# Token mixer: four sequences' values in four quarters of TensorE's array, softmax denominators from halves that GpSimd adds

## What is computed

```python
q, k, v = jnp.split(qkv, 3, axis=1)              # each 128 x 32 x 512
scale = 1.0 / np.sqrt(np.sqrt(ch))
weight = jnp.einsum('bct,bcs->bts', q * scale, k * scale)
weight = jax.nn.softmax(weight.astype(jnp.float32), axis=-1)
h = jnp.einsum('bts,bcs->bct', weight, v)
```

## Time and profile before

| what | us |
|---|---|
| median of 3 runs | 2330.69 (2326.32 to 2330.86) |
| the profiled execution | 2332.05 |
| its span in the profile | 2330.2 |
| PE busy / DVE busy / ACT busy / POOL busy | 2230.4 / 1630.9 / 1523.8 / 1080.4 |
| first and last value matmul of the mixer | 32.2 and 537.7 |

### The profile page before, as it was taken

The page is one execution under the profiler, slowest core; times in us unless marked ns, Lnnn a source line. Parts: engine busy times, 40 slices in busy tenths (PEclk is TensorE's granted clock), DMA queues, the critical chain, the costliest instruction groups (busy, mean ns, idle before and its releaser), DMA issues. The chain is left out here.

```text
span 2330.2 us, 41583 instructions
## 1 busy us (share of the span) xinstructions
PE 2230.4 (96%) x13316; PEld 1135.3 (49%) x13316; DVE 1630.9 (70%) x2893; ACT 1523.8 (65%) x2430; POOL 1080.4 (46%) x1045
## 2 busy tenths in 40 slices
PE   7999999998999998899999999999998999999997
PEld 2333333334666665444444444666664444444443
DVE  6666666674788989666667633666666787788775
ACT  4666666666788787445556423766675777777775
POOL 1322223236877778322324401444454566666654
PEclk9999999998999999999999999999999999999999
DMA  5555555441334221312222212222221011111111
GB/s 141 138 138 131 130 135 133 128 129 50 102 129 129 69 74 63 103 48 80 75 88 95 75 50 68 78 81 81 81 82 42 23 50 51 41 50 41 42 37 63
DMA packets 144303, 194.97 MB, mean 84 GB/s; under 512 B 32773, under 2 KB 76261, under 8 KB 144154
## 3 DMA queue, kind: packets, MB, share of 16 engines
q1 hardware_dynamic: 115642, 154.79, 22.1%
q10 hardware_dynamic: 28512, 38.28, 5.9%
HBM read 125.10 MB, written 42.21 MB: 72 GB/s over the span
## 5 line engine op out<-in xcount | busy, mean ns | idle before, releaser
L341 DVE TENSOR_REDUCE tm_negmax<-tm_s 128x1 f32<-128x512 f32 x512 | 323.6, 679 | 159.3 <-PE tm_s L384 158.9
L2222 PE MATMUL f_bank<-f_xs,gu 128*128 128x512 f16 x1408 | 417.0, 379 | 1.6 <-ACT f_firstg L2048 1.1
L303 ACT ACTIVATE tm_prob<-tm_s 128x1024 f32<-128x1024 f32 x256 | 257.6, 1023 | 132.4 <-PE tm_s L404 126.6
L2250 PE MATMUL f_bank<-dn,f_ghi 128*128 128x512 f16 x704 | 265.5, 379 | 1.9 <-DVE f_glo L2157 1.9
L421 PE MATMUL tm_o<-tm_prob,tm_vt 128*64 128x512 f32 x1024 | 255.7, 620 | 0.0
L384 PE MATMUL tm_s<-tm_qk 96*128 96x512 f16 x512 | 200.6, 394 | 27.2 <-DMA tm_qk<-tm_xs 15.6
L2012 POOL TENSOR_TENSOR f_firstg<-f_firstg,f_secondg 128x512 f32<-128x512 f32 x88 | 152.3, 1730 | 153.1 <-DVE f_secondg L2141 153.1
L2222 PEld LDWEIGHTS f_bank<-f_xs,gu 128*128 128x128 f16 x1408 | 135.9, 98 | 162.8 <-ACT f_firstg L2048 1.5
L264 POOL TENSOR_TENSOR tm_hn<-tm_nd,tm_rows 128x1024 f32<-128x1024 f32 x32 | 75.2, 2351 | 289.1 <-DMA tm_rows<-rden 289.1
L404 PE MATMUL tm_s<-tm_qk 98*128 98x512 f16 x512 | 194.6, 384 | 0.3 <-DMA tm_qk<-tm_mrow 0.2
L987 PE MATMUL a_bankB<-a_wo,a_yThi 128*128 128x512 f16 x512 | 155.5, 386 | 0.0
(11 more groups left out here) (193 smaller groups left out, 5648.1 us busy)
## 6 DMA issues: line engine op xcount, KB each, us to landing
tm_qk<-tm_xs SPq DMA_DIRECT2D x384, 64.0 KB, 2.1
tm_xqk<-in_qk ACTq DMA_DIRECT2D x32, 512.0 KB, 4.6
a_hin<-h SPq DMA_DIRECT2D x64, 256.0 KB, 2.6
a_hres<-h SPq DMA_DIRECT2D x64, 256.0 KB, 3.0
h<-a_hout SPq DMA_DIRECT2D x64, 256.0 KB, 2.6
f_hin<-h SPq DMA_DIRECT2D x64, 256.0 KB, 2.9
f_hres<-h SPq DMA_DIRECT2D x64, 256.0 KB, 2.9
tm_vt<-in_vt ACTq DMA_DIRECT2D x32, 256.0 KB, 3.1
```

What stands on the lines that cost most here:

```text
L303: nc.scalar.activation(prob[b][:, 2 * h:2 * h + 2, :], s2[:, i % 2, :, :], ACT.Exp, scale=SCALE).then_inc(exp_done, 1)
L341: nc.vector.tensor_reduce(negmax[u][:, m:m + 1], s1[:, p % BANKS, :], AX.X, ALU.max, negate=True).then_inc(s1_read, 1)
L2222: last = nc.tensor.matmul(bank_of(m, i)[:, :], (gate, up)[which][:, j, m * P:(m + 1) * P], xs[g % 2][:, x, j, :], start=x == 0, stop=x == 1)
L2250: last = nc.tensor.matmul(pz[i][:, :], gparts[x][:, (MT * g + m) % RING, i * P:(i + 1) * P], down[w][:, m, :], start=m == 0 and c % 3 == 0 ...
```

## The change

- Values: `vt` loses its columns of ones and becomes 32 columns wide. All four sequences have a column quarter of the array each. A tile has 16 value matmuls as before, now in four blocks, one per key block j, of four matmuls each; they stand at g = 14 and at g = 0, 2 and 4 of the next step.
- Denominators: GpSimd adds the halves of each `prob` (key blocks 0 and 1 to 2 and 3) into `added`, four additions of 128x1024 per tile. Eight more fp32 matmuls per tile (`sum_probs`), with a 32-column tile of ones, sum them over the keys, in two blocks of four at g = 8 and 10 of the next step. They write bank 2 of `s1`. The table `BANK` keeps first scores out of that bank between place 4 and place 13, so places 5 to 12 have banks 0 and 1 alone.
- `o` is copied once per tile, the sums' bank once per tile (still two copies on ScalarE).
- The normalisation moves from GpSimd (128x1024) to VectorE (128x512), in place in `nd`, behind g = 10 of the step after next; the reciprocal moves from g = 12 to g = 1 of the step after.
- The denominators' DMAs and the rows' become one per tile each, and the store one; the order of SyncE's queue changes. Four memsets at the start are replaced by a small one.
- An exponential now waits for the addition that reads its tile, and an addition for the sums of the tile before.

```diff
+    BANK = (1, 2, 0, 1, 2, 0, 1, 0, 1, 0, 1, 0, 1, 2, 0, 1, 2, 0)
+    SUMS_BANK, FIRST_BEHIND_SUMS = 2, 13
-    vt = [sb(f"tm_vt{i}", [P, NT, 2 * C, B], F32) for i in range(2)]
+    vt = [sb(f"tm_vt{i}", [P, NT, C, B], F32) for i in range(2)]
+    ones = sb("tm_ones", [P, C], F32)
...
-    VALUES_AT = {7: 0, 11: 1, 15: 2, 3: 3}
+    VALUES_AT = {14: (0, 0), 0: (1, 1), 2: (1, 2), 4: (1, 3)}
+    SUMS_AT = {8: 0, 10: 1}
+    BEFORE = [max(q for q in range(p - USES, p) if BANK[q % USES] == BANK[p]) for p in range(USES)]
...
         def step(k, u):
             n = 2 * k + u
             stack(n + 1, 1 - u, 2)
+            stack(n + 1, 1 - u, 3)
+            inverses(n - 2, u, k - 1)
+            maxima(n, u, 1)
             inverse_rows(n - 2, u, k - 1)
-            stack(n + 1, 1 - u, 3)
-            maxima(n, u, 1)
-            denominators(n - 1, 1 - u)
             stack(n + 2, u, 0)
             stack(n + 2, u, 1)
             maxima(n + 1, 1 - u, 0)
-            inverses(n - 1, 1 - u, k + u - 1)
+            denominators(n - 1, 1 - u)
...
+        def add(t, b):
+
+            if inside(t, TILES):
+                wait(pool, exp_done, 8 * t + (3, 4, 7, 8)[b])
+                wait(pool, sums_done, t)
+                pool.tensor_tensor(added[b][:, :, :], prob[b][:, 0:2, :], prob[b][:, 2:4, :], ALU.add)\
+                    .then_inc(added_done, 1)
 
         def step(k, u):
             n = 2 * k + u
-            normalise(n - 2, u, k - 1)
+            add(n - 1, 2)
+            add(n - 1, 3)
             x_lo(n + 3, 1 - u)
+            add(n, 0)
+            add(n, 1)
...
-                if i % 2 == 0:
-                    wait(act, pv_done, 4 * (t - 1) + i // 2 + 1)
+                if i % 4 < 2:
+                    wait(act, added_done, 4 * (t - 1) + b + 1)
+                if i in (0, 2):
+                    wait(act, pv_done, 4 * (t - 1) + i + 2)
...
-                if i == 1:
-                    sums_out(n - 1, 1 - u, 1)
                 if i == 2:
+                    copy_values(n - 1, 1 - u, k + u - 1)
                     load_values(n + 1, 1 - u)
                 if i == 3:
                     x_hi(n + 3, 1 - u, k + 1 + u)
                 if i == 4:
+                    copy_sums(n - 1, 1 - u)
                     load(n + 4, u)
-                if i == 5:
-                    sums_out(n, u, 0)
...
+        def normalise(t, u, half):
+
+            if inside(t, TILES):
+                wait(dve, rows_in[u], 16 * (half + 1))
+                nc.vector.tensor_tensor(nd[u][:, 0, :], nd[u][:, 0, :], rows[u][:, :], ALU.mult)\
+                    .then_inc(norm_done, 1)
...
                 maxes(n + ahead, (u + ahead) % 2, m)
-                if g == 12:
-                    inverse_sums(n - 1, 1 - u, k + u - 1)
-        return step
+                if g == 1:
+                    inverse_sums(n - 2, u, k - 1)
+                if g == 10:
+                    normalise(n - 2, u, k - 1)
...
                 wait(pe, s1_read, freed(t, place(m)))
-                nc.tensor.matmul(s1[:, place(m) % BANKS, :], qk[u][0:KS, 0, b, i * P:(i + 1) * P],
+                if place(m) == FIRST_BEHIND_SUMS:
+                    wait(pe, sums_out, t - 1)
+                nc.tensor.matmul(s1[:, BANK[place(m)], :], qk[u][0:KS, 0, b, i * P:(i + 1) * P],
...
+                for b in range(B):
+                    last = nc.tensor.matmul(o[C * b:C * (b + 1), :], vt[u][:, j, :, b], prob[b][:, j, :],
+                                            start=j == 0, stop=j == NT - 1)
                 last.then_inc(pv_done, 1)
...
+                out = sums_bank(t)
+                for b in range(B):
+                    last = nc.tensor.matmul(out[C * b:C * (b + 1), :], ones[:, :], added[b][:, j, :],
+                                            start=j == 0, stop=j == 1)
```

More of the change, by code:

```diff
@@ L390, in maxima @@
                 p = turned(pair)
-                wait(pe, s1_read, use(t, place(HALF * pair + HALF - 1)) + 1)
-                nc.tensor.transpose(s1[0:HALF, p % BANKS, 0:P], negmax[u][:, HALF * pair:HALF * (pair + 1)],
+                wait(pe, s1_read, freed(t + pair, p))
+                nc.tensor.transpose(s1[0:HALF, BANK[p], 0:P], negmax[u][:, HALF * pair:HALF * (pair + 1)],
                                     ident[:, :]).then_inc(s1_ready, 1)
@@ L1109, in _ @@
         run(step, 2, 2)
+        run(step, 3, 4)
         store(30)
         store(31)
-        run(step, 3, 4)
         mixer.before.all_rows(sp)
@@ L1171, in _ @@
         run(step, -3, -3)
-        run(mix, 32, 32)
-        run(step, -2, 0)
+        copy_values(31, 1, 15)
+        run(step, -2, -2)
+        copy_sums(31, 1)
+        run(step, -1, 0)
         for n in range(1, 29):
@@ L1203, in _ @@
     def _(pe):
-        mix = mixer.tensor(pe)
+        mix, sum_probs = mixer.tensor(pe)
         prepare, step = att.tensor(pe)
@@ L1211, in _ @@
         run(mix, 32, 32)
-        run(step, -2, 0)
+        run(step, -2, -2)
+        sum_probs(31, 0)
+        sum_probs(31, 1)
+        run(step, -1, 0)
         rows_read, normalise, _, _ = ternary.tensor(pe)
```

150 lines of the change are left out of this document (82 added, 68 removed).

## The result

The changed kernel takes 2464.32 us (2462.77 to 2466.93, 4 runs) against 2330.78 in the runs beside it: 1.0578 times as long, 95% interval 1.056 to 1.0597, 133.5 us slower. The forecast was 2336, range 2294 to 2364. It was wrong.

What follows compares the result with a forecast made beforehand. PE was taken to set the mixer's pace at 16.04 us a tile. Blocks -36, banks +10, normalisation +32 and start -0.6 gave +5.6 on 2332.05; with the median 1.4 lower, 2336 us, range 2294 to 2364.

Steps and rivals of the forecast that it cites:

- Blocks: PE's value and sum matmuls: six blocks of 1.16 us against four of 2.02, -1.1 us a tile, -36 in all.
- The forecast's estimate from the factor in the Trainium skill: Rival on PE's blocks: four streams slow each other by a third, a block of 1.42, +50, 2386 us, chance 0.03.
- Two banks: First scores at g = 5 to 8 wait for maxima: 0.45 us a tile, +0.3 net, +10 in all.
- GpSimd's hold of VectorE: VectorE's normalisation waits 1.25 us for GpSimd's low part, delaying the transposed maxima: 1.1 to 1.2 us a tile, +32.
- The denominators' way: Copy, DMA, reciprocal, DRAM, rows: starts up to half a step later, normalisation almost a step later too; costs nothing.
- the normalisation's term: VectorE's normalisation behind g = 10, just before transpose T of g = 11: +32 in all; bounds 0 and 2.1 a tile.
- the forecast's own case: Blocks' saving given back through VectorE's wait for GpSimd: 2336 us, by itself 2322 to 2350, chance 0.42.
- the second rival: The maxima's DMA round trip, 4.2 to 5.0 us against 4.3, comes late at g = 8: 2352 us, chance 0.16.
- The handover: End of the mixer: two normalisations leave POOL, the last tile's additions come; 0, bounds -5 and +5.
- a sign of being wrong: Forecast wrong as a whole if PE waits for `added_done` or stages behind the mixer move over 5 us.

Runs made afterwards that it cites:

- run 2: Changed kernel with VectorE's normalisation multiplying by a constant tile of ones, not waiting for the rows' DMA of its own tile: 2350.8 us (1.0099).
- run 6: Changed kernel with the rows written by four DMAs, one per sequence, in place of one over all 128 partitions: 2351.9 us (1.0104).
- run 3: Changed kernel with GpSimd's additions cut to 32 columns in place of 1024: 2377.8 us (1.0212).
- run 4: Changed kernel with twelve matmuls that nobody reads ahead of the first score of g = 13, where TensorE stops: 2404.3 us (1.0322).
- run 1: Changed kernel with VectorE's normalisation behind the maximum of g = 13 in place of g = 10: 2353.0 us (1.0098).
- run 10: Run 9 with SyncE's queue writing the last tile's inverses behind the loads of attention's step 2, no longer ahead of them: 2328.1 us (1.0002).
- run 9: Run 1 with the load of queries and keys issued behind the exponential of i = 6 instead of i = 4: 2332.9 us (1.0009).
- run 18: Run 10 with the store, the load of queries and keys, and the last of attention's weight loads behind the exponential of i = 7: 2320.0 us (0.9961).

## Why the prediction was wrong

**Right.** Blocks of 1.12 (forecast 1.16, "since the halves overlap without any loss"). The forecast's estimate from the factor in the Trainium skill (TensorE: Matmul & The Clock Gate, Part 3) was 1.42; the measurement decides against carrying that factor over to these four fp32 quarters. Two banks: 0.29 + 0.15 = 0.44 at g = 7 and 8 (0.45 forecast). GpSimd's hold of VectorE as a mechanism: runs 2 and 6 have it exactly, a normalisation of 1.9 us ending behind the low part. It was over-priced: a stop of 0.66, not 1.1 to 1.2.

**The step that failed** is one sentence: "The denominators' way (copy, DMA, reciprocal, DRAM, rows) starts up to half a step later but the normalisation is almost a step later too. Nothing." It was not costed by a single row. The new rows' DMA is another one than before (one over 128 partitions in place of two over 32 with twice the length), and lands 6.1 us after its issue starts instead of 2.9, at T + 1.6 where it is wanted at T - 0.3. Being late by 1.9 then costs 1.3 more, since GpSimd's additions have begun (run 3), and the stop of 3 us costs 2.1 more through the clock (run 4). The upper bound of the normalisation's term, "2.1, a whole low part", assumed that it is held by one operation of GpSimd from the moment it is asked for. The clock stood in no term at all: every stop had been priced at its own length. Altogether 5.3 us a tile in 28 tiles, 148, less the 0.86 x 32 = 28 that the blocks and banks really gave: 120 of the 123 us.

**Without that step** the forecast's own case is run 6: 2352 instead of 2336. Its tile takes 16.53 us where the forecast's sum gives 16.04 + 5.6 / 32 = 16.2; that is 10 of the 16 us. Another 1.1 come in the mixer (its last value matmul starts 17.2 us later than before, where 5.6 and 10.5 make 16.1) and 1.7 behind it; the other 3 stay open. The handover is not the rest. Two waits more than pay for the cheaper hold: the maxima's DMAs are waited for 0.7 us a tile (the second rival, which I had taken as an alternative to my case; it comes on top of it, and at g = 0), and a first score at g = 12 waits 0.3 us for the sums' copy out of the lent bank (309.23 to 309.77), which was in no term.

**The handover**, "0, bounds -5 and +5", cost 7.5, and with the 3.2 behind it the stages after the mixer moved by 10.7, over the 5 that the forecast had named as a sign of being wrong. Why the 7.5 is open. The queue position in SyncE's tail is a part at most: runs 1 and 6 have the same position, and the stretch from the last value matmul to the first ternary weight load takes 469.8 and 467.2 us there, against 468.7 before and 476.2 in the changed kernel; moving it (run 10 against run 9) gave 3.3. The stretch behind it is 2.9 to 3.3 us longer in runs 1, 6, 9, 10 and 18 as well; the cause was not looked for.

## What to carry to other kernels

When a wait moves to an engine that others wait for, cost the whole way of the data it waits for, from a row for each hop; a DMA whose shape changes is a new hop, even with the same bytes. Price a stop of TensorE twice, by its length and by what runs at half clock behind it if the clock falls, which the length alone did not decide here. Look for the point at which a late arrival misses a gap and meets the next operation. When a matmul loop gets shorter, the DMAs of two kilobytes that it hides get no shorter: list what is queued ahead of them, in the issuing queue and in the engines.
